# A two-layer decoder: the latent attention's context work made in the first phase and brought back from memory

## The chip, the core and the metric

The kernel runs on one core of a Trainium2 chip. The metric is the device time of one execution in microseconds (us). TensorE's granted clock has two levels, 1.2 and 2.4 GHz; the profile writes it as a share of 2.4 GHz.

## The reference, cut to what matters

Sixty-four sequences of 128 rows of 256 numbers go through two layers. What bears on the change is the attention of a second-layer sublayer, in which the running activations ask a context:

```python
x = x + mamba(layernorm(x)); x = x + cross_attention(layernorm(x), ctx)      # ctx's own keys and values
x = x + experts(layernorm(x)); x = x + causal_attention(layernorm(x))
x = x + latent_attention(ctx, layernorm(x)); x = x + ternary_layer(layernorm(x))

def latent_attention(ctx, latents):
    xn = layer_norm(ctx, ln_x_w, ln_x_b)              # depends on ctx alone
    ln = layer_norm(latents, ln_l_w, ln_l_b)
    k, v = split(concat([xn, ln]) @ Wkv)              # 8 heads of 64
    q, k = l2norm(ln @ Wq) * q_scale, l2norm(k) * k_scale
    p = softmax(where(mask, (q @ k.T) * 8, -max))
    return layer_norm((p @ v) @ Wo, ln_o_w, ln_o_b)
```

The context's half of keys and values depends on nothing that the layers compute, so it can be made at any time.

## The kernel before

The work runs in three phases. **Phase 1** loops over the 64 sequences: the state-space sublayer (chains M, V, N), the first cross attention (Y makes the context's keys and values for it, X the rest), and the router with the shared expert (F). **Phase 2** goes through 144 tiles of routed rows, expert by expert. **Phase 3** loops over the sequences again: causal attention (A), the context's norm, keys and values for the latent attention (C), the latents' norm, queries, keys and values (K), the latent attention (L), and the last part (T).

Every engine runs the same loop body over and over. A chain is a generator that stops at named steps, and a table, `ORDER`, gives for each phase and engine the order in which the steps of all chains stand in one body: "Kla0" is step la0 of chain K. Chains have depths, as `("A", A, 0), ("C", C, 1)`: in the body in which A works on sequence n, C works on sequence n-1. A body is thus one sequence's worth of each chain, 67 or so bodies make a phase, and 60 of them are the hardware loop. Engines take their steps strictly in the table's order; a step that waits holds up all that is behind it on its engine. Semaphores tie the engines together: `done(engine, name, b)` waits for a signal of sequence b, `was(...)` for the same signal of the sequence before (a buffer that has to be free).

Chain C has, in the kernel before, these steps in phase 3, all on PSUM bank Q[3]: moments of the context rows on VectorE (lnc), 1/sqrt of the variance on GpSimd, the normed rows on VectorE (lncn), two transposes on TensorE and two scaled copies on ScalarE; keys = two matmuls of 512 columns (la1, la1h), their squares on ScalarE (lq0), sums by head on VectorE, a power on GpSimd, the scaling on VectorE (lu0), four transposes (lT0) and a copy into `klT`; values = two more matmuls of 512 columns (la3, la3h) and a copy into `Vl`. Each float32 matmul of the source shows as two instructions in the trace. Chain K does the same for the latents on Q[4] and feeds the same two tiles.

Other names used below: in phase 1, "Nd0" to "Nd3" are subtractions on GpSimd over 128x1024 elements (L618), "Nm0" to "Nm2" products on VectorE of the same size (L847), "Nm3" the fourth of them on GpSimd (L622); "Vcv" to "Vcv3" are the convolution, 16 small operations on VectorE (L817, L819), "Vcth" the tanh after it on ScalarE; "Ftop" is the choice of two experts on VectorE (from L893), "Frk" the rank matmuls that wait for it, "Xs0" and "Xs2" the scores of the cross attention, "Xm0" to "Xm3" their maxima and exponentials, "Xt2" and "Xt3" the transposes of the exponentials and the copies (L1162), "Xpv" the products with the values (L1440), "Nx1" the sum that ends the state-space sublayer (L861).

## Time and profile before

| | us |
|---|---|
| median of 3 runs | 4805.45 (4796.27 to 4813.17) |
| profiled execution | 4825.85 |
| its span, first to last instruction | 4824.2 |
| mean granted TensorE clock | 0.956 |

The 40 slices of the page show phase 1 up to about 2510 us, phase 2 to about 2800 us, and phase 3 from there to the end. In phase 1 TensorE is busy for eight tenths of nearly every slice, in phase 3 for nine tenths or more. "PE" is TensorE, "PEld" its weight loads, "DVE" VectorE, "ACT" ScalarE, "POOL" GpSimd and "SP" SyncE; "PEclk" is the granted clock.

### The profile page before, as it was taken

The numbers are of one execution on the slowest core, as the hardware profiler recorded it, in microseconds if no ns is written. First come the engines' busy times: TensorE is split into PE (matmuls) and PEld (weight loads), VectorE is DVE, ScalarE is ACT, GpSimd is POOL, SyncE is SP. The second block draws the span as 40 slices with busy tenths as digits, with TensorE's granted clock in tenths as the row PEclk, the third lists the DMA queues.
The fourth block names the chain that finished last, engine by engine and source line by source line (L and its number), as shares of the span: only waits on it lengthen the run. The fifth ranks groups of instructions, "written<-read, shape, count | busy, mean of one in ns | idle before, by whom it ended". The sixth has DMA issues, their size and how long they took to land. (4 is left out here: it accounts for less than half of the span.)

```text
span 4824.2 us, 120433 instructions
## 1 busy us (share of the span) xinstructions
PE 4196.8 (87%) x34006; PEld 3000.4 (62%) x34071; DVE 3385.8 (70%) x8668; ACT 2902.8 (60%) x7030; POOL 2741.4 (57%) x4093
## 2 busy tenths in 40 slices
...
DMA packets 215885, 304.09 MB, mean 63 GB/s; under 512 B 56608, under 2 KB 167456, under 8 KB 215840
## 3 DMA queue, kind: packets, MB, share of 16 engines
...
q8 instruction: 23, 0.38, 0.0%
q14 instruction: 22, 0.18, 0.0%
...
## 5 line engine op out<-in xcount | busy, mean ns | idle before, releaser
L1402 PE MATMUL Q<-ident,arena 128*128 128x128 f32 x4768 | 824.8, 298 | 141.0 <-ACT arena L1145 48.9
L1402 PEld LDWEIGHTS Q<-ident,arena 128*128 128x128 f32 x4768 | 570.3, 149 | 385.2 <-issue 135.8
L1397 PE MATMUL Q<-Wkvl,arena 128*128 128x512 f32 x1024 | 498.7, 599 | 0.0
L618 POOL TENSOR_TENSOR arena<-arena 128x1024 f32<-128x1024 f32 x256 | 479.6, 1890 | 6.7 <-DMA arena<-cum_rows 6.7
L682 POOL TENSOR_TENSOR l<-l,half_pow 128x8 f32<-128x8 f32 x192 | 318.8, 1661 | 230.4 <-DVE l L1025 228.8
L707 POOL TENSOR_TENSOR arena<-arena,part_of 128x512 f32<-128x512 f32 x256 | 264.1, 1043 | 188.6 <-DVE part_of L1063 187.7
L769 DVE TENSOR_REDUCE mx<-Q 128x4 f32<-128x512 f32 x512 | 343.8, 681 | 9.3 <-PE Q L1425 4.7
L1440 PE MATMUL Q<-arena 128*17 128x128 f32 x4096 | 243.2, 313 | 102.3 <-ACT arena L1162 102.2
L1431 PE MATMUL Q<-ident,arena 128*128 128x128 f32 x2048 | 300.0, 280 | 23.3 <-ACT arena L1162 18.4
L1431 PEld LDWEIGHTS Q<-ident,arena 128*128 128x128 f32 x2048 | 231.9, 141 | 132.3 <-issue 93.6
L1155 ACT ACTIVATE arena<-Q,mx 128x128 f32<-128x128 f32 x1024 | 282.6, 374 | 0.5 <-DVE mx L769 0.5
L1425 PE MATMUL Q<-arena 32*128 32x128 f32 x4096 | 281.9, 276 | 0.0
L1202 ACT ACTIVATE arena<-arena 128x1024 f32<-128x1024 f32 x256 | 268.6, 1049 | 0.1
L1199 ACT ACTIVATE arena<-arena 128x1024 f32<-128x1024 f32 x256 | 268.1, 1047 | 0.0
L1425 PEld LDWEIGHTS Q<-arena 32*128 32x128 f32 x4096 | 262.8, 189 | 3.2
L1361 ACT ACTIVATE arena<-Q,mxl 128x256 f32<-128x256 f32 x512 | 235.8, 473 | 46.2 <-DVE mxl L1058 38.9
L1497 PE MATMUL Q<-arena 128*16 128x128 f32 x4096 | 164.3, 278 | 107.6 <-DVE arena L847 98.1
L1440 PEld LDWEIGHTS Q<-arena 128*17 128x17 f32 x4096 | 146.4, 106 | 178.2 <-issue 163.8
L1162 ACT ACTIVATE arena<-Q 128x512 f32<-128x512 f32 x384 | 220.0, 589 | 56.6 <-PE Q L1431 55.8
L847 DVE TENSOR_TENSOR arena<-arena 128x1024 f32<-128x1024 f32 x192 | 233.2, 1242 | 2.9 <-ACT arena L1202 2.9
L1397 PEld LDWEIGHTS Q<-Wkvl,arena 128*128 128x128 f32 x1024 | 169.6, 190 | 103.8 <-issue 103.6
L819 DVE SCALAR_TENSOR_TENSOR arena<-arena,convw 128x128 f32<-128x128 f32 x768 | 225.8, 356 | 6.8
...
## 6 DMA issues: line engine op xcount, KB each, us to landing
arena<-cum_rows SPq DMA_DIRECT2D x256, 512.0 KB, 6.3
arena<-routed_rows SPq DMA_DIRECT2D x144, 128.0 KB, 2.1
expert_rows<-arena POOLq DMA_DIRECT2D x144, 128.0 KB, 2.0
arena<-in_x_dram SPq DMA_DIRECT2D x128, 128.0 KB, 5.1
arena<-in_ctx_dram SPq DMA_DIRECT2D x128, 128.0 KB
x_rows<-arena SPq DMA_DIRECT2D x128, 128.0 KB, 1.7
arena<-x_rows SPq DMA_DIRECT2D x128, 128.0 KB, 2.4
out_dram<-arena SPq DMA_DIRECT2D x64, 128.0 KB, 1.7
```

What stands on the lines that cost most here:

```text
L618: tell(g.tensor_tensor(E8[j], E8[j], cums[:, 8 * j:8 * j + 8].unsqueeze(2).broadcast_to([P, 8, T]), ALU.subtract), "diff")
L682: link(pool, c, b, g.tensor_tensor(l2[:, k, :], l2[:, k, :], half_pow[:, :], ALU.pow), bare=True)
L707: tell(g.tensor_tensor(both, both, part_of[:, 2 * k:2 * k + 2].unsqueeze(2).broadcast_to([P, 2, 2 * T]), ALU.mult), "Pln")
L769: largest = v.tensor_reduce(mx[:, 4 * j:4 * j + 4], pj, AX.X, ALU.max, negate=True)
L1155: last = s_.activation(S[:, j, g, :], banks[j][:, g * T:(g + 1) * T], ACT.Exp, bias=mx[:, 4 * j + g:4 * j + g + 1])
L1199: tell(s_.activation(Ew[j], Ew[j], ACT.Abs), "gap")
L1202: tell(s_.activation(Ew[j], Ew[j], ACT.Exp, scale=-1.0), "E")
L1397: last = mm(out, lhs(c), rhs(c), start=c == 0, stop=c == n - 1)
L1402: last = nc.tensor.transpose(out[:, c * P:(c + 1) * P], src[:, c * P:(c + 1) * P], ident[:, :])
L1425: last = mm(banks[j][:, g * T:(g + 1) * T], QT[r, g, :], KT[r, g // 2, :], start=False, stop=g == NG - 1)
L1431: last = nc.tensor.transpose(bank[:, g * T:(g + 1) * T], S[:, j, g, :], ident[:, :])
L1440: last = mm(bank[32 * (h % 4):32 * (h % 4) + AW + 1, h // 4 * T:(h // 4 + 1) * T], V[:, h, :], PT[:, j, g, :], start=True, stop=True)
```

## The change

All of chain C moves from phase 3 to phase 1, at depth 2, and shares bank Q[2] with chain Y there. Its keys and values are stored to two new arrays in memory by a new chain S on SyncE, one body later, and loaded in phase 3 straight into `klT` and `Vl` by two new steps of L on SyncE. The host also hands over the context with its last two axes swapped, and Y loads that in place of transposing the rows: TensorE's step YcT and ScalarE's are gone. Wkvl's load moves from the later weights to the first ones. In `ORDER` C's steps are put into phase 1 and taken from phase 3, and other steps of phase 3 change places. TensorE's step "Mcum" waits for one signal in place of another before its idle matmuls.

```diff
     1: {
         "SP": """
-            Ncb0 Ncb1 Ncb2 Yc Xm Mx Ncb3 Nx Mco Fm Fo
+            Ncb0 Ncb1 Ncb2 Sk Sv Yc Cc Xm Mx Ncb3 Nx Mco Fm Fo
         "POOL": """
-            Nd0 Nd1 Nd2 Xx1r Fln3 Xln2 Mln1 Nd3 Msp Nm3 Fsc Nyg Nrms
+            Nd0 Nd1 Nd2 Xx1r Fln3 Xln2 Mln1 Clnc Nd3 Msp Nm3 Clq0 Fsc Nyg Nrms
         "DVE": """
-            Fln3 Xln2 Nm0 Mln1 Fr Yk Ftop Mdt Fslot Msp Xm0 Xm1 Fhg Nm1 Nm2 Xm2 Xm3 Fxo Vcv Vcv1 Vcv2 Vcv3 Ny0 Vxs2 Ny1 Vcb Vxdt Vgz Nx1 Xho
+            Fln3 Xln2 Clnc Nm0 Mln1 Fr Yk Clncn Ftop Mdt Fslot Msp Xm0 Xm1 Fhg Nm1 Nm2 Xm2 Xm3 Clq0 Fxo Vcv Vcv1 Vcv2 Clu0 Vcv3 Ny0 Vxs2 Ny1 Vcb Vxdt Vgz Nx1 Xho
         "ACT": """
-            Ng0 YcT Ne0 Ng1 Fln3 Xln2 Fln3n Xmr Xln2n Mln1 Frx Mln1n Xq Mab Vbc Ne1 Ng2 Yv Fth Ne2 Ng3 FhT Ne3 Xm0 Xm1 Vxp Xm2 Mcum Xm3 NYt0 Xt0 NYt1 Xt1 Vcth Xt2
-            Xt3 Nsq XOT NyT Vtz
+            Ng0 Ne0 Ng1 Fln3 Xln2 Fln3n Xmr Xln2n Mln1 Frx Mln1n Xq Yv Mab Vbc Ne1 Ng2 Clncn Fth Ne2 Ng3 FhT Ne3 Xm0 Xm1 Vxp Clq0 Xm2 Mcum Xm3 NYt0 Xt0 NYt1 Xt1
+            ClT0 Vcth Xt2 Xt3 Nsq XOT Cla3 NyT Vtz
         "PE": """
-            YcT Yk Nv0 Fln3n Yv Xln2n Fr Mln1n Xq Vbc Mdt Frk Xs0 Fgu Fguh Vip1 Vip1h FhT Xs2 Fdn Mcum Nv1 Nv2 Xt0 Nv3 Xt1 Ny0 Xt2 VCB Ny1 Xt3 Xpv Xpv0 VxsT Xpv1
-            Xpv2 NyT Xpv3 Vz Vzh Npr Nprh XOT
+            Yk Nv0 Fln3n Yv Xln2n Fr Mln1n Xq Vbc Mdt Frk Xs0 Clncn Fgu Fguh Vip1 Vip1h FhT Cla1 Xs2 Cla1h Fdn Mcum Nv1 Nv2 Xt0 Nv3 Xt1 Ny0 Xt2 VCB Ny1 ClT0 Xt3
+            Xpv Xpv0 VxsT Xpv1 Xpv2 Cla3 NyT Xpv3 Cla3h Vz Vzh Npr Nprh XOT
     3: {
         "SP": """
-            Ax Cc Kx Lm Tx To
+            Ax Lk Lv Kx Lm Tx To
         "POOL": """
-            Ag Kx4c Kln5 Aln4 Kln6 Clnc Tlno Tln7 Klq1 Lp0 Lp1 Lp2 Clq0 Lp3 Klq2
+            Ag Kx4c Kln5 Kln6 Aln4 Tlno Tln7 Klq1 Lp0 Lp1 Lp2 Lp3 Klq2
         "DVE": """
-            Kln5 Clnc Ax3 Aln4 Kln5n Kln6 Aln4n Lmr Kln6n Tlno Clncn Tx5 Tln7 Lm0 Lm1 Taq Klq1 Ak Lm2 Lm3 Lp0 Lp1 Klu1 Am0 Am1 Am2 Am3 Lp2 Tx6 Clq0 Lp3 At0 Lt0
-            At2 Klq2 Clu0 Lt2 Aho Klu2 Ax4
+            Kln5 Ax3 Kln5n Kln6 Lmr Aln4 Kln6n Tlno Lm0 Aln4n Tx5 Tln7 Lm1 Klq1 Taq Ak Lm2 Klu1 Lm3 Lp0 Am0 Lp1 Am1 Am2 Lp2 Lp3 Am3 Lt0 At0 Tx6 Klq2 At2 Lt2 Klu2
+            Aho Ax4
         "ACT": """
-            Aln4n Kln6n Clncn Lp0 Lp1 Klq1 Aq TaT Lp2 Lp3 KlT1 Am0 Clq0 Am1 Am2 Am3 At1 Klq2 At3 Lt1 AOT Lt3 AoT ClT0 KlT2 Llo Cla3 Kla4
+            Kln6n Aln4n Klq1 Lp0 Lp1 Aq Lp2 TaT KlT1 Lp3 Am0 Klq2 Am1 Am2 Am3 At1 Lt1 At3 AOT Lt3 AoT KlT2 Llo Kla4
         "PE": """
-            Two Twoh Aln4n Ls0 Kln6n Aq Clncn Kla0 Kla0h Aqv Ak Cla1 Ls2 TaT As0 Ttern KlT1 Cla1h Lt0 As3 Lt1 Kla2 At0 At1 Kla2h At2 At3 Apv Apv0 Apv1 Apv2 Apv3
-            Lt2 Lt3 AOT Lpv0 AoT ClT0 KlT2 Apr Lpv1 Cla3 Cla3h Kla4 Kla4h
+            Two Twoh Ls0 Kln6n Kla0 Aln4n Kla0h Aq Aqv Ak Ls2 TaT As0 KlT1 Ttern Kla2 Kla2h As3 Lt0 Lt1 At0 Lt2 At1 At2 At3 Apv Apv0 Apv1 Apv2 Apv3 Lt3 AOT Lpv0
+            AoT KlT2 Apr Lpv1 Kla4 Kla4h
...
+    kl_d = nc.dram_tensor("context_keys", (NB, P, KV), F32)
+    vl_d = nc.dram_tensor("context_values", (NB, P, KV), F32)
...
+        sqc, vlc = part(512), part(512)
+        xnc, cT = sqc[:, 0:D], cut(vlc[:, 0:D], DC)
...
@@ SyncE, phase 1
+            chunks(Wkvl, wkv1)
             counts["w_first"] = n_w
...
             def Y(b):
                 yield "c"
-                was(sp, "ctxTps", b)
+                was(sp, "v0", b)
+                tell(sp.dma_start(ctxT, ctxt_d[bass.ds(b, 1)].rearrange("a (c p) t -> p (a c) t", p=P)), "ctxT_in", 16)
+
+            def C(b):
+                yield "c"
+                was(sp, "lnc_xn", b)
                 tell(sp.dma_start(ctx0, rows(ctx_d, b)), "ctx0_in", 16)
+
+            def S(b):
+                yield "k"
+                done(sp, "klT0", b)
+                tell(sp.dma_start(rows(kl_d, b), sqc), "kl_out", 16)
+                yield "v"
+                done(sp, "Vl0", b)
+                tell(sp.dma_start(rows(vl_d, b), vlc), "vl_out", 16)
...
-            program(sp, "SP", 1, (("M", M, 0), ("N", N, 1), ("Y", Y, 2), ("X", X, 2), ("F", F, 3)))
+            program(sp, "SP", 1, (("M", M, 0), ("N", N, 1), ("Y", Y, 2), ("C", C, 2), ("X", X, 2), ("F", F, 3), ("S", S, 3)))
...
@@ SyncE, phase 3
             def L(b):
+                yield "k"
+                was(sp, "Sl", b, 4)
+                tell(sp.dma_start(klT[:, :, 0:T], cut(rows(kl_d, b), 4)), "kl_in", 16)
+                yield "v"
+                was(sp, "PVl", b)
+                tell(sp.dma_start(Vl[:, 0, :], rows(vl_d, b)), "vl_in", 16)
...
@@ VectorE, phase 1
+            def C(b):
+                yield "lnc"
+                done(dve, "ctx0_in", b, 16)
+                moments("lnc", ctx0, stC, mvC, "C_DVE", b)
+                yield "lncn"
+                done(dve, "lnc_rstd", b)
+                was(dve, "kl_out", b, 16)
+                tell(v.tensor_scalar(xnc, ctx0, mvC[:, 0:1], mvC[:, 3:4], ALU.subtract, ALU.mult), "lnc_xn")
+                yield from total(0, sqc, b)
+                yield from unit(0, "kn0", sqc, Q[2], b)
...
@@ ScalarE, phase 1
-                yield "cT"
-                done(act, "ctxTps", b)
-                tell(s_.activation(ctxT, cut(Q[2][:, 0:D], DC), ACT.Copy), "ctxT")
...
+            def C(b):
+                yield "lncn"
+                was(act, "vl_out", b, 16)
+                copyT("lnc", Q[2], cT, b, lnx)
+                yield "lq0"
+                done(act, "la1", b)
+                tell(s_.activation(sqc, Q[2][:, :], ACT.Square), "latsq0")
+                yield "lT0"
+                done(act, "kT0", b)
+                tell(s_.activation(sqc, Q[2][:, :], ACT.Copy), "klT0")
+                yield "la3"
+                done(act, "la3", b)
+                tell(s_.activation(vlc, Q[2][:, :], ACT.Copy), "Vl0")
...
@@ TensorE, phase 1
                 yield "cum"
-                done(pe, "ln1_T", b)
+                done(pe, "dt_pre", b)
                 awake(Q[0][:, 0:2 * T], 5)
...
-                yield "cT"
-                done(pe, "ctx0_in", b, 16)
-                was(pe, "v0c", b)
-                was(pe, "k0c", b)
-                tell(transposes(Q[2], ctx0, DC), "ctxTps")
                 yield "k"
-                done(pe, "ctxT", b)
+                done(pe, "ctxT_in", b, 16)
+                was(pe, "Vl0", b)
                 tell(across_heads(Q[2], Wk0, ctxT), "k0")
...
+            def C(b):
+                con = lambda c: cT[:, c, :]
+                yield "lncn"
+                done(pe, "v0c", b)
+                done(pe, "k0c", b)
+                lnT("lnc", xnc, Q[2], b)
+                yield "la1"
+                done(pe, "lnc_T", b)
+                last = yield from halves("la1", Q[2][:, :], con, lambda c: Wkvl[:, c, 0:KV])
+                tell(last, "la1")
+                yield "lT0"
+                done(pe, "kn0", b)
+                tell(transposes(Q[2], sqc, 4), "kT0")
+                yield "la3"
+                done(pe, "klT0", b)
+                last = yield from halves("la3", Q[2][:, :], con, lambda c: Wkvl[:, c, KV:2 * KV])
+                tell(last, "la3")
...
@@ the same functions C are taken out of phase 3 on every engine; TensorE's L waits for the loads
-                done(pe, "klT0", b)
+                done(pe, "kl_in", b, 16)
...
-                        done(pe, "Vl0", b)
+                        done(pe, "vl_in", b, 16)
```

## Rows read from the trace of the kernel before

**Rows 1.** The page, part 1: busy time, share of the span and instructions of each engine.
```profile
PE 4196.8 (87%) x34006; PEld 3000.4 (62%) x34071; DVE 3385.8 (70%) x8668; ACT 2902.8 (60%) x7030; POOL 2741.4 (57%) x4093
```

**Rows 2.** Busy time of each engine over the loop bodies of phases 1 and 3.
```profile
201.80:2416.80 2215.00, 1815.90 (x15759) 1313.82 (x15812) 1558.43 (x4131) 1441.15 (x3128) 1414.39 (x2125) 0.94 0.25 79
...
2926.90:4733.70 1806.80, 1787.00 (x14397) 1247.56 (x14396) 1427.71 (x3422) 1117.85 (x2951) 1033.59 (x1475) 1.00 0.11 31
```

**Rows 3.** SyncE, one instruction in each loop body: first and last start, in us.
```profile
L437 SPq MOVE cum_rows<-arena x60: 29/29/29, 201.8 to 2416.8; - x60
...
L525 SPq MOVE out_dram<-arena x60: 29/29/29, 2926.9 to 4733.7; - x60
```

**Rows 4.** Waits in phase 1: who for whom, total us, times, longest.
```profile
PE Q L1440 <- ACT arena L1162: 98.6, 59, 2.5
...
PE Q L1497 <- DVE arena L847: 91.6, 59, 1.6
```

**Rows 5.** TensorE in order of time in phase 3: start us, us, group, idle before.
```profile
3626.28 3.70 PE L1397 MATMUL Q<-Wkvl,arena 128*128 128x512 f32 x8
...
3629.82 1.89 PE L1397 MATMUL Q<-Wol,arena 128*128 128x256 f32 x8
...
3633.24 0.44 PE L1402 MATMUL Q<-ident,arena 128*128 128x128 f32 x2
...
3634.41 0.38 PE L1402 MATMUL Q<-ident,arena 128*128 128x128 f32 x2
...
3634.63 1.93 PE L1397 MATMUL Q<-Wql,arena 128*128 128x512 f32 x4
...
3642.66 0.66 PE L1402 MATMUL Q<-ident,arena 128*128 128x128 f32 x4 [0.28 <-DVE arena L1030]
...
3643.15 1.02 PE L1397 MATMUL Q<-Wkvl,arena 128*128 128x512 f32 x2
```

**Rows 6.** ScalarE in order of time in phase 3.
```profile
3633.72 0.81 ACT L1140 ACTIVATE arena<-Q,lnl 128x128 f32<-128x128 f32 x2 [1.37 <-PE Q L1402]
```

**Rows 7.** Groups of instructions in phase 3: busy us, mean ns of one, idle before.
```profile
L682 POOL TENSOR_TENSOR l<-l,half_pow 128x8 f32<-128x8 f32 x177 | 293.9, 1661 | 199.3 <-DVE l L1025 197.8
...
L1030 DVE TENSOR_TENSOR arena<-Q,l 128x512 f32<-128x512 f32 x177 | 120.0, 678 | 0.0
...
L1025 DVE TENSOR_REDUCE l<-arena 128x8 f32<-128x512 f32 x177 | 119.9, 677 | 1.5 <-ACT arena L1339 1.5
...
L758 DVE BATCH_NORM_STATS2 stK<-arena 128x6 f32<-128x256 f32 x118 | 50.5, 428 | 8.9
```

**Rows 8.** VectorE in order of time in phase 1.
```profile
1117.79 0.48 DVE L861 SCALAR_TENSOR_TENSOR arena<-Q,ss,arena 128x256 f32<-128x256 f32 x1 [0.70 <-PE Q L1397]
...
1121.10 1.23 DVE L847 TENSOR_TENSOR arena<-arena 128x1024 f32<-128x1024 f32 x1
...
1126.30 0.57 DVE L894 TENSOR_TENSOR rt<-rt 128x16 f32<-128x16 f32 x1
...
1138.57 3.24 DVE L817 SCALAR_TENSOR_TENSOR arena<-arena,convw,convb 128x128 f32<-128x128 f32 x4
...
1141.84 3.55 DVE L819 SCALAR_TENSOR_TENSOR arena<-arena,convw 128x128 f32<-128x128 f32 x12
```

**Rows 9.** GpSimd in order of time in phase 1, the same body.
```profile
1124.95 1.90 POOL L618 TENSOR_TENSOR arena<-arena 128x1024 f32<-128x1024 f32 x1
...
1138.98 2.42 POOL L622 TENSOR_TENSOR arena<-arena 128x1024 f32<-128x1024 f32 x1
```

**Rows 10.** TensorE in order of time in phase 1, the same body.
```profile
1146.78 0.65 PE L1440 MATMUL Q<-arena 128*17 128x128 f32 x8 [1.74 <-ACT arena L1162]
```

**Rows 11.** A stretch of phase 1: busy time, granted clock, DMA share, GB/s.
```profile
1147.40:1150.80 3.40, 3.40 (x31) 2.21 (x32) 1.29 (x2) 0.48 (x2) 3.32 (x4) 0.52 0.97 347
```

**Rows 12.** SyncE in order of time in phase 1: the context load's issue.
```profile
1107.40 0.51 SPq L454 DMA_DIRECT2D arena<-in_ctx_dram  x1
```

**Rows 13.** DMA issues in phase 1: KB each, median us to landing.
```profile
arena<-in_x_dram SPq DMA_DIRECT2D x118, 128.0 KB, 3.9
```

More of the change, by code:

```diff
@@ L225, in two_layers @@
         S1, PT1 = (part(2048).rearrange("p (j g k) -> p j g k", j=4, g=NG) for _ in range(2))
-        ctx1, xnc, l5, xn6, x4c, x4t = (part(D) for _ in range(6))
-        cT, lT = cut(part(D), DC), cut(part(D), DC)
-        sqc, sql, qn = part(512), part(512), part(512)
-        kn = part(1024).rearrange("p (c n) -> p c n", c=2)
+        l5, xn6, x4c, x4t = (part(D) for _ in range(4))
+        lT = cut(part(D), DC)
+        sql, qn, kn = part(512), part(512), part(512)
         qlT, klT, Vl = cut(part(512), 4), part(1024).rearrange("p (m t) -> p m t", m=4), part(1024).rearrange("p (c n) -> p c n", c=2)
@@ L268, in two_layers @@
         Q = [ctx.enter_context(nc.psum_tensor(f"Q{i}", [P, 512], F32)) for i in range(8)]
-        for n in ("xa_in", "xr_in", "cum_out", "wide0", "wide1", "wide2", "wide3", "ctx0_in", "mask0_in", "meta_out", "xo_out", "meta_in", "x2s_in", "ctx1_in", "mask1_in", "x4_out", "x4t_in", "out_done"):
+        for n in ("xa_in", "xr_in", "cum_out", "wide0", "wide1", "wide2", "wide3", "ctx0_in", "mask0_in", "meta_out", "xo_out", "meta_in", "x2s_in", "mask1_in", "x4_out", "x4t_in", "out_done", "ctxT_in", "kl_out", "vl_out", "kl_in", "vl_in"):
             sig(n, 16)
@@ L501, in A @@
                 tell(sp.dma_start(x2s, rows(x2_d, b)), "x2s_in", 16)
-            def C(b):
-                yield "c"
-                was(sp, "lnc_xn", b)
-                tell(sp.dma_start(ctx1, rows(ctx_d, b)), "ctx1_in", 16)
             def K(b):
```

113 lines of the change are left out of this document (41 added, 72 removed).

## The prediction

> **What bounds the kernel now.** I read the page first: TensorE is busy for 87% of the span, more than any other engine [rows 1]. An average over three phases doesn't say what a stage is worth, so next come the windows over the two loops. In phase 3 TensorE is busy for 1787 of 1807 us, at the full clock: work taken from it there shortens the body, unless something else ends later. In phase 1 it is busy for 1816 of 2215 us at a granted clock of 0.94 (part of that busy time is itself slow), and VectorE, ScalarE and GpSimd stand at 70%, 65% and 64% [rows 2]: no engine is full, so a chain that crosses the engines must be the bound. The first and last of 60 instructions that stand once in each body give the periods: (2416.8 - 201.8) / 59 = 37.54 us in phase 1, (4733.7 - 2926.9) / 59 = 30.62 us in phase 3, 30.5 in an ordinary body [rows 3]. In phase 1 TensorE waits 1.6 us in each body for VectorE's product (Nm0) and as much for ScalarE's copies (Xt3) [rows 4].
>
> The sum is thus a race: 64 passes of chain C leave a loop that TensorE fills, and enter one that is bound by waits.
>
> **Phase 3.** In the order of TensorE's starts, eight instructions of 512 columns take 3629.82 - 3626.28 = 3.54 us; half of those are Cla3, and Cla1 is as many: 3.54 us in all. The two transposes of Clncn take 0.22 us (3634.41 to 3634.63), four transposes as in KlT1 0.49, which I take for ClT0. With gaps C costs 4.3 us of TensorE in each body, and 0.28 us of waiting for VectorE stands in it too [rows 5]. What VectorE, ScalarE and GpSimd lose by it (VectorE some 2.3 us: moments, norm, sum, scaling) was beside TensorE's work. TensorE's own work then is 30.5 - 0.3 - 4.3 = 25.9 us.
>
> The cover goes as well. Now Kla0 comes 1.4 us after the start of its transposes (3633.24 to 3634.63), and Aq and Clncn fill that time [rows 5]: ScalarE's two copies begin 0.48 us after the transposes' start and take 0.81 [rows 6]. In the new order Kla0 stands right behind Kln6n, so TensorE waits there: 3633.72 + 0.81 + 0.1 - (3633.24 + 0.27) = 1.1 us. That is a new wait that nothing in the table hides. Following the other steps through the new table in the same way I find four smaller ones: As0 behind k1c (0.15), Ttern and Kla2 behind ScalarE, which must finish Lp2 first (0.6), AOT behind the copy of the heads (0.3), Apr behind the copy of o1 (0.4); 1.5 us together at worst, none at best. I take half, as the row with the only wait of today's body (0.28) lies between. New body: 25.9 + 1.1 + 0.8 = 27.8, which is 2.7 us less. Bounds: 1.8 less (all waits and some more) to 4.6 less (none). The two loads from memory and the lost context load are SyncE's: Lv waits for the body's last product (Lpv1) with Kx, Lm and Tx behind it, but Kx waited that long before, for x4. 64 x 2.7 = 173 us saved (115 to 294).
>
> **Phase 1.** I lay the body out from Nx1 at 1117.79 (time 0) [rows 8]. One path goes round: x1, the norms, router, Ftop, rank, Xs0, then VectorE without a pause from Xm0 to the end of the convolution, tanh, Xt3, Xpv, and TensorE without a pause to the next Nx1. What stands on it counts in full; what stands beside it is free.
>
> - Clnc: two operations of 0.43 and 0.18 with a gap, 0.7 us [rows 7], ahead of Nm0, for which TensorE already waits [rows 4, 8]. The later Nv0 pushes Fr by 0.6 us: **+0.6**.
> - Clncn: one operation, near 0.42 us, ahead of Ftop. Its time comes just when GpSimd makes Nd3. The row shows what that does: L894, an operation on 16 columns, began at 1126.30 and took 0.57, to the very end of Nd3 at 1124.95 + 1.90 = 1126.85 [rows 8, 9]. Nd3 stood at 7.2 on my clock and is 0.8 us later by Clnc on GpSimd (an addition and a power), so it ends at 9.9; then comes Clncn, to 10.3, and L894 ends at 10.7 in place of 9.1: with the 0.6 above 1.6 us late, so **+1.0** more (0.4 if the two don't meet).
> - Clncn's transposes and Cla1 on TensorE go ahead of Xs2, 1.2 us of which VectorE's late arrival at Xm2 covers most: **+0.4**. Cla1h is beside the path.
> - Clq0: 0.68 us [rows 7] on VectorE between Xm3 and the convolution, and 0.3 us until ScalarE's square, which stands behind Vxp, is there: **+1.0**.
> - The first four convolution operations took 3.24 us, where twelve more of their size take 3.55 together, so 2.0 of it is a stall: they met GpSimd's Nm3 (2.42 us) [rows 8, 9]. In the new order VectorE gets there later against Nm3, and half of that stall goes: **-1.0** (0 to -2.0).
> - Clu0: 0.68 us [rows 7] ahead of Vcv3: **+0.7**. GpSimd's power for it takes 1.66 us [rows 7], behind Nm3, in the shadow of Vcv1 and Vcv2; the scatter behind it has slack.
> - ClT0 on ScalarE, ahead of Vcth: it ends 0.3 us after the convolution: **+0.3**.
> - Cla3 and Cla3h: four instructions by 0.443 us, between Xpv and Npr, where TensorE is never idle: **+1.8**.
> - The lost YcT is worth nothing: TensorE waits for Nm0 right after.
>
> Sum: 4.8 us in each body, 64 x 4.8 = 307 us (bounds: 2.0 with the stall gone and the small terms hidden, 6.5 with further slow clock).
>
> A page bears on two of these terms. The Trainium skill (SBUF — State Buffer, "Who interferes with whom") says that VectorE with two inputs in SBUF, or in a fast mode on one, and GpSimd reading SBUF lock each other out for a whole instruction; L894's row agrees. By that page Clncn, a scalar operation from SBUF to SBUF, is locked out as L894 was, and the sum is the 4.8 above; were it not, the term would be 0.4 and the sum 4.2.
>
> SyncE in phase 1: Sv waits for Vl0, made by the last steps of the body before, some 3.4 us ahead of Nx1. Behind it stand Yc, Cc, Xm, Mx and Ncb3; Yc's place was at 1107.40, 10.4 us ahead [rows 12]. So these loads now start 7 us later. A load of x takes 3.9 us in the median to land [rows 13]; the context would be there 1 to 2 us after Nx1, its moments are due at 3.3, x is due at 5.2, wide3 at 8.1. All hold, by 1 to 3 us. I cost it at nothing; if that cover is gone, VectorE waits in the path, 1 to 2 us a body.
>
> Wkvl among the first weights: the same bytes through the same engines ahead of phase 1, +1 us. The store of the last keys is waited for before phase 3, long done.
>
> **Sum.** 4825.85 - 173 + 307 + 1 = 4961 us against the profiled execution, which stands 20 us above the median; 135 us more than before, so 4940 us as a median.
>
> **The rivals.**
>
> *Phase 1 absorbs it (faster).* TensorE idles for 37.5 - 30.8 = 6.8 us in a body [rows 2, 3], more than C's 4.3. If the small insertions on VectorE fall into waits, only Cla3's 1.8 us are left: 64 x 1.8 = 115, sum 4805 - 173 + 115 + 1 = 4750. It decides when phase 1's body grows by less than 2.7 us. For it: VectorE is idle for 30% of the body. Against it: those idle times are not between Xm0 and the convolution's end.
>
> *The clock.* After the wait of 1.74 us before Xpv [rows 10] TensorE ran at 0.52 in the following 3.4 us, just in the stretch without a pause [rows 11], which costs about 1.7 us. Longer waits (Nv0's, Frk's and the one ahead of ClT0 each grow by 1 us or more) may add another such stretch: +1.5 a body, 5035 us. The Trainium skill (TensorE: Matmul & The Clock Gate, "HAM oscillation — how this bites in real kernels") tells of loops that fall back to the low clock in each pass through a wait; no row here shows it for these places. The other way, Cla3 and ClT0 fill enough to keep the clock high before Npr: -1.7 a body, 4830 us.
>
> *Phase 3 takes no new wait.* TensorE stays as full as now: -294 us, sum 4819.
>
> *The held queue.* Sv's wait makes the loads late by 1.5 us: +96, 5035 us.
>
> **How the numbers follow.** The forecast (4850 to 5000) has 0.42; phase 1 absorbs it 0.23; a further slow stretch 0.12, the slow stretch lost 0.07; phase 3 clean 0.08; held queue 0.08. A measurement of this kernel tells about 0.3%, 14 us, from no change. Faster: 0.23 and some of the two near 4820 make 0.28; within 0.3%: 0.07; slower 0.65. The range takes in the absorbing case down to its 4730 and both cases at 5035: 4730 to 5060; the likeliest one's own is 4850 to 5000.
>
> **What would show it.** In the changed profile: phase 3's body near 27.8 us, with a wait of 1.1 us before Kla0 on ScalarE's scaled copies; phase 1's body near 42.3, Clncn's operation near 1 us long at GpSimd's L618, L817's four shorter than 3.24 us together, TensorE still without a pause from Xpv to Npr, and TensorE's wait for the rank (L1570) up from 1.0 to over 2 us. A phase 1 body under 40.2 us makes the prediction wrong; so would waits on DMA in phase 1.

## The result, and the profile after

The changed kernel takes 5262.45 us in the median of four runs (5256.60 to 5263.77), the kernel before 4808.87 in the same rounds: a ratio of 1.0944, 95% interval 1.0927 to 1.0960. Forecast were 4940 us and a range of 4730 to 5060. The direction was right; the size was not, and the time lies outside the range.

The page, part 1, of the changed kernel, to be set beside [rows 1]:

```profile
PE 4419.7 (84%) x33878; PEld 3103.7 (59%) x33943; DVE 3295.9 (63%) x8668; ACT 2851.9 (54%) x6966; POOL 2763.9 (53%) x4093
```

TensorE has the same work less YcT, and is busy for 223 us longer: part of its work runs slower. The windows over the loops say where (columns as in [rows 2]: window, its length, busy time of PE, PEld, DVE, ACT and POOL, granted clock, DMA share, GB/s):

```profile
217.20:2688.00 2470.80, 2053.76 (x16467) 1468.73 (x16520) 1604.19 (x4426) 1558.42 (x3364) 1571.71 (x2361) 0.92 0.28 87
3209.40:5168.00 1958.60, 1758.25 (x13572) 1190.98 (x13571) 1293.81 (x3126) 953.26 (x2656) 898.07 (x1239) 0.92 0.14 40
```

The granted clock of phase 3 was 1.00 and is 0.92. The first and last of the two instructions that stand once in each body, as in [rows 3]:

```profile
L441 SPq MOVE cum_rows<-arena x60: 29/29/29, 217.2 to 2688.0; - x60
```

```profile
L545 SPq MOVE out_dram<-arena x60: 29/29/29, 3209.4 to 5168.0; - x60
```

Phase 1's body is (2688.0 - 217.2) / 59 = 41.88 us, 4.34 more than before (forecast: 4.8 more). Phase 3's is (5168.0 - 3209.4) / 59 = 33.20 us, **2.58 more** (forecast: 2.7 less). 64 x (4.34 + 2.58) = 443 us, and the profiled spans differ by 5262.1 - 4824.2 = 438: the two bodies are the whole of it. The error sits in phase 3.

**Phase 3.** The chain of waits of TensorE in the loop of phase 3 (total us, times, longest):

```profile
PE Q L1756 <- DVE mrow L1078: 105.7, 59, 3.6
PE Q L1417 <- ACT arena L1164: 53.0, 59, 0.9
PE Q L1417 <- ACT arena L1363: 26.7, 59, 0.5
```

The second is the wait before Kla0, 53.0 / 59 = 0.9 us a body where 1.1 was forecast; the third is Kla2's, 0.45, one of the "smaller ones". The first is new: in each of 59 bodies the scores Ls0 wait for the mask's row, 105.7 / 59 = 1.8 us. Who made that row late is seen by following one body through three engines. SyncE:

```profile
4030.94 0.59 SPq L530 DMA_DIRECT2D arena<-context_keys  x1
4036.55 0.34 SPq L533 DMA_DIRECT2D arena<-context_values  x1
4037.19 0.36 SPq L525 DMA_DIRECT2D x_rows<-arena  x1
4037.81 0.34 SPq L536 DMA_DIRECT2D mask1i<-in_mask_BxS_bk_dram  x1
```

VectorE, which turns the mask into mrow (L1078):

```profile
4041.39 0.29 DVE L1078 TENSOR_SCALAR mrow<-mask1i 128x256 bf16<-128x256 uint8 x1 [2.16 <-DMA mask1i<-in_mask_BxS_bk_dram]
```

TensorE:

```profile
4036.44 1.98 PE L1417 MATMUL Q<-Wkvl,arena 128*128 128x512 f32 x4
4038.26 1.89 PE L1417 MATMUL Q<-Wol,arena 128*128 128x256 f32 x8
4041.74 0.39 PE L1756 MATMUL Q<-mrow,onesb 1*128 1x512 bf16 x2 [1.59 <-DVE mrow L1078]
4042.06 1.46 PE L1761 MATMUL Q<-arena 64*128 64x256 f32 x8
...
4045.03 2.07 PE L1417 MATMUL Q<-Wql,arena 128*128 128x512 f32 x2 [0.90 <-ACT arena L1164]
```

SyncE issues the keys' load at 4030.94 and then stands for 5.0 us, until 4036.55: the values' load (L533) waits for Lpv1, the last reader of the old values. The store of x4 and the mask's load (L536) come after it, at 4037.19 and 4037.81. The mask lands some 3.5 us later; VectorE has been idle for 2.16 us and TensorE for 1.59 us by then. There is more in these rows than the wait: two products of Wql take 2.07 us at 4045.03, which take 1.13 where the mask is in time (e1, below). The clock in that stretch, and ahead of it:

```profile
4043.00:4046.00 3.00, 2.10 (x7) 0.79 (x4) 2.64 (x8) 0.81 (x2) 1.18 (x3) 0.50 0.00 0
```

```profile
4041.00:4042.00 1.00, 0.26 (x2) 0.09 (x2) 0.61 (x2) 0.00 (x0) 0.00 (x0) 1.00 0.07 24
4043.00:4044.00 1.00, 1.00 (x6) 0.29 (x2) 0.82 (x4) 0.00 (x0) 0.85 (x3) 0.50 0.00 0
```

So the clock had already fallen when the wait of 0.90 us began, at 4044.13: it falls behind the wait for the mask.

The kernel before shows whether the mask became late or was needed sooner:

```profile
3627.53 0.33 SPq L516 DMA_DIRECT2D mask1i<-in_mask_BxS_bk_dram  x1
```

```profile
3631.86 0.39 PE L1739 MATMUL Q<-mrow,onesb 1*128 1x512 bf16 x2
```

Counted from the products with Wkvl (3626.28 before [rows 5], 4036.44 after), the mask's load was issued at 1.25 and is issued at 1.37 us, nearly the same. Ls0 began at 5.6 us; without the wait it would now begin at 3.7 (4041.74 - 1.59 = 4040.15).

**Phase 1.** One body from L881 (the old L861, time 0, at 1027.58) to the next at 1068.90; 41.32 us, where the body of [rows 8] takes 37.33 (the next L861 starts at 1155.12). VectorE:

```profile
1031.46 1.23 DVE L867 TENSOR_TENSOR arena<-arena 128x1024 f32<-128x1024 f32 x1
...
1036.53 0.17 DVE L909 TENSOR_REDUCE rt<-Q 128x1 f32<-128x16 f32 x1 [3.18 <-PE Q L1410]
1037.08 0.93 DVE L961 TENSOR_SCALAR arena<-arena,mvC 128x256 f32<-128x256 f32 x1
...
1038.11 0.17 DVE L914 TENSOR_TENSOR rt<-rt 128x16 f32<-128x16 f32 x1
...
1046.58 0.42 DVE L935 SCALAR_TENSOR_TENSOR arena<-arena,Q 128x256 f32<-128x256 f32 x1 [1.15 <-ACT arena L1281]
...
1050.23 1.29 DVE L789 TENSOR_REDUCE mx<-Q 128x4 f32<-128x512 f32 x2 [0.50 <-PE Q L1445]
1051.92 0.69 DVE L947 TENSOR_REDUCE l<-arena 128x8 f32<-128x512 f32 x1 [0.40 <-ACT arena L1292]
...
1052.86 1.13 DVE L837 SCALAR_TENSOR_TENSOR arena<-arena,convw,convb 128x128 f32<-128x128 f32 x4
...
1056.37 0.69 DVE L952 TENSOR_TENSOR arena<-Q,l 128x512 f32<-128x512 f32 x1
```

L909 is the router's first operation. In the body before it stands as:

```profile
1125.30 0.17 DVE L889 TENSOR_REDUCE rt<-Q 128x1 f32<-128x16 f32 x1 [2.30 <-PE Q L1390]
```

GpSimd and TensorE in the same body of the changed kernel:

```profile
1031.52 1.22 POOL L602 TENSOR_TENSOR mvX<-mvX,eps 128x1 f32<-128x1 f32 x1
...
1035.96 1.90 POOL L638 TENSOR_TENSOR arena<-arena 128x1024 f32<-128x1024 f32 x1
```

```profile
1032.74 1.06 PE L1517 MATMUL Q<-arena 128*16 128x128 f32 x16 [2.88 <-DVE arena L867]
...
1034.21 1.71 PE L1410 MATMUL Q<-Wv,arena 128*128 128x256 f32 x4
...
1042.66 3.46 PE L1417 MATMUL Q<-Wsgu,arena 128*128 128x512 f32 x4
1045.96 1.95 PE L1410 MATMUL Q<-arena,Win 128*128 128x128 f32 x16
...
1060.03 0.62 PE L1460 MATMUL Q<-arena 128*17 128x128 f32 x8 [1.81 <-ACT arena L1186]
...
1061.96 1.12 PE L1417 MATMUL Q<-Wkvl,arena 128*128 128x512 f32 x2
```

### The profile page after: what moved, and what is told of

It reads as the page before. It is cut to its first block, busy times and chain, and to the rows that moved or that the text cites. A ratio compares the mean times of both kernels' runs of the same rounds, so it can differ in the third digit from the quotient of the medians.

```text
span 5262.1 us, 120973 instructions
## 1 busy us (share of the span) xinstructions
PE 4419.7 (84%) x33878; PEld 3103.7 (59%) x33943; DVE 3295.9 (63%) x8668; ACT 2851.9 (54%) x6966; POOL 2763.9 (53%) x4093
## 4 chain that ended last, share of the span: by engine, by line
PE 67%; DVE 11%; issue 8%; DMA 5%; ACT 4%; POOL 2%; SPq 1%; DVEq 1%; POOLq 0%; ACTq 0%
PE Q L1417 19%; PE Q L1422 12%; PE Q L1410 11%; PE Q L1445 4%; DMA mask1i<-in_mask_BxS_bk_dram 4%; PE Q L1451 4%; PE Q L1460 3%; PE Q L1761 3%; PE Q L1517 2%; PE Q L1632 2%; DVE arena L867 1%; PE Q L1644 1%; PE Q L1794 1%; PE Q L1756 1%; POOL arena L714 1%
## 5 line engine op out<-in xcount | busy, mean ns | idle before, releaser
L1422 PE MATMUL Q<-ident,arena 128*128 128x128 f32 x4640 | 817.2, 295 | 128.8 <-ACT arena L1169 49.0
L1422 PEld LDWEIGHTS Q<-ident,arena 128*128 128x128 f32 x4640 | 549.5, 148 | 442.2 <-issue 185.4
L1417 PE MATMUL Q<-Wkvl,arena 128*128 128x512 f32 x1024 | 537.8, 627 | 29.5 <-ACT arena L1363 29.4
L672 POOL TENSOR_TENSOR l<-l,half_pow 128x8 f32<-128x8 f32 x192 | 332.4, 1731 | 367.0 <-DVE l L947 364.9
L638 POOL TENSOR_TENSOR arena<-arena 128x1024 f32<-128x1024 f32 x256 | 479.8, 1891 | 7.4 <-DMA arena<-cum_rows 7.3
L789 DVE TENSOR_REDUCE mx<-Q 128x4 f32<-128x512 f32 x512 | 343.6, 682 | 103.9 <-PE Q L1445 103.9
L1517 PE MATMUL Q<-arena 128*16 128x128 f32 x4096 | 178.0, 296 | 188.6 <-DVE arena L867 188.5
L1460 PE MATMUL Q<-arena 128*17 128x128 f32 x4096 | 215.2, 276 | 106.9 <-ACT arena L1186 106.9
L1451 PE MATMUL Q<-ident,arena 128*128 128x128 f32 x2048 | 295.3, 277 | 3.1 <-ACT arena L1179 2.4
L1417 PE MATMUL Q<-Wql,arena 128*128 128x512 f32 x256 | 234.6, 1017 | 57.5 <-ACT arena L1164 57.5
L947 DVE TENSOR_REDUCE l<-arena 128x8 f32<-128x512 f32 x192 | 131.1, 683 | 194.8 <-ACT arena L1359 168.8
L1410 PEld LDWEIGHTS Q<-arena,Win 128*128 128x128 f32 x1536 | 217.6, 217 | 56.4 <-issue 52.2
L1517 PEld LDWEIGHTS Q<-arena 128*16 128x16 f32 x4096 | 110.2, 100 | 237.8 <-DVE arena L867 220.0
L1451 PEld LDWEIGHTS Q<-ident,arena 128*128 128x128 f32 x2048 | 230.0, 141 | 31.8 <-issue 26.2
```

The lines of the kernel that those rows point to most:

```text
L638: tell(g.tensor_tensor(E8[j], E8[j], cums[:, 8 * j:8 * j + 8].unsqueeze(2).broadcast_to([P, 8, T]), ALU.subtract), "diff")
L672: link(pool, c, b, g.tensor_tensor(l2[:, k, :], l2[:, k, :], half_pow[:, :], ALU.pow), bare=True)
L789: largest = v.tensor_reduce(mx[:, 4 * j:4 * j + 4], pj, AX.X, ALU.max, negate=True)
L1410: last = mm(out, lhs(c), rhs(c), start=c == 0, stop=c == n - 1)
L1417: last = mm(out, lhs(c), rhs(c), start=c == 0, stop=c == n - 1)
L1422: last = nc.tensor.transpose(out[:, c * P:(c + 1) * P], src[:, c * P:(c + 1) * P], ident[:, :])
```

## The experiments

They ran on three chips (e1 to e4, e5 to e8, e9 to e12), on each of which the kernel before took 4827 to 4830 us; each ratio is to the kernel before on the same chip. "P1" and "P3" are the periods of the two bodies, worked out as above; "clock" is the granted clock over the loop of phase 3 (for e6 to e8: of phase 1).

| kernel | us | ratio to before, 95% | P1 | P3 | clock |
|---|---|---|---|---|---|
| e5, the changed kernel again | 5242.1 | 1.0853 (1.0835 to 1.0871) | 41.87 | 32.96 | 0.92 |
| e1, mask's load early | 4954.6 | 1.0263 (1.0246 to 1.0280) | 41.04 | 29.06 | 1.00 |
| e2, values' load late | 5144.2 | 1.0652 (1.0634 to 1.0669) | 41.08 | 32.00 | 0.94 |
| e3, old order of phase 3 | 5063.4 | 1.0487 (1.0469 to 1.0504) | 41.08 | 30.70 | 0.96 |
| e4, e3 and mask early | 5052.3 | 1.0470 (1.0448 to 1.0492) | 41.04 | 30.52 | 0.97 |
| e10, TensorE kept busy | 5074.0 | 1.0505 (1.0487 to 1.0522) | 41.07 | 30.94 | 0.99 |
| e9, e1 and Ls0 between | 4962.2 | 1.0272 (1.0255 to 1.0290) | 41.04 | 29.24 | 1.00 |
| e6, e1 and values' products last | 4879.7 | 1.0111 (1.0094 to 1.0128) | 39.75 | 29.10 | 0.97 |
| e7, e1 and moments later | 4941.5 | 1.0233 (1.0216 to 1.0250) | 40.78 | 29.08 | 0.94 |
| e8, e1 and norm later | 5070.7 | 1.0505 (1.0487 to 1.0522) | 42.86 | 29.10 | 0.90 |
| e11, e6, e7 and e9 together | 4887.1 | 1.0121 (1.0104 to 1.0138) | 39.94 | 29.18 | 1.00 |
| e12, before with turned context | 4827.0 | 0.9995 (0.9986 to 1.0005) | 37.55 | 30.62 | 1.00 |

**The theory** after the result: in phase 3 the mask's load is too late for Ls0, which the new order puts ahead of Aln4n and with C's products no longer in front; the idle time then brings the clock down. **Rivals**: the hand-made order of steps is bad by itself; or the loads of keys and values are late.

**e1_mask_early.** The mask's load goes ahead of the values' load and of x4's store.

```diff
-            Ax Lk Lv Kx Lm Tx To
+            Ax Lk Lm Lv Kx Tx To
```

> The changed kernel with one move on SyncE in phase 3: the mask's load (Lm) goes ahead of the load of the values (Lv) and the store of x4 (Kx). Theory 'late mask': VectorE's 2.2 us wait for the mask, TensorE's 1.6 us wait behind it and the slow clock after it go; phase 3's body falls from 33.2 to 29 to 30 us, the time to 5000 to 5080 us. Rival 'the new order of steps': the body is bound by the steps' order, the mask's wait turns into another, and the time stays within 40 us of 5262.

SyncE in phase 3 of e1:

```profile
4016.79 0.39 SPq L533 DMA_DIRECT2D mask1i<-in_mask_BxS_bk_dram  x1
4021.54 0.33 SPq L536 DMA_DIRECT2D arena<-context_values  x1
4022.18 0.36 SPq L525 DMA_DIRECT2D x_rows<-arena  x1
```

The waits of TensorE over its loop of phase 3:

```profile
PE Q L1417 <- ACT arena L1164: 52.9, 59, 0.9
PE Q L1417 <- ACT arena L1363: 26.6, 59, 0.5
PE Q L1756 <- DVE mrow L1078: 3.0, 2, 2.7
```

and TensorE in time, around Kla0:

```profile
4025.39 1.14 PE L1761 MATMUL Q<-arena 64*128 64x256 f32 x8
...
4027.79 1.13 PE L1417 MATMUL Q<-Wql,arena 128*128 128x512 f32 x2 [0.90 <-ACT arena L1164]
...
4036.98 1.98 PE L1417 MATMUL Q<-Wkvl,arena 128*128 128x512 f32 x4 [0.45 <-ACT arena L1363]
```

The mask is issued 5.4 us ahead of x4's store, mrow is waited for twice in 59 bodies, the clock is back at 1.00, and the same two products of Wql take 1.13. The body goes from 32.96 (e5) to 29.06. The time was forecast at 5000 to 5080 us and comes out lower, since phase 1, whose code is the same, has 0.8 us less a body as well; that part is looked at under e6. In phase 3 that one row of the table of steps is worth 3.9 us a body, some 240 us of the 415 that the change costs (e5); the two profiles differ by 242 us behind the end of phase 1's loop and by 49 ahead of it. Forecast for phase 3's body had been 27.8; more on the other 1.26 below.

With the mask in time the change costs 127 us, where the prediction had 135. That this is so close is luck: 29.06 + 41.04 and the forecast 27.8 + 42.3 are both 70.1, with phase 3 1.3 us above its forecast and phase 1 as much below.

**e2_values_late.** Values' load behind the store and the mask (`Ax Lk Kx Lm Lv Tx To`).

> The changed kernel with the load of the values (Lv) moved on SyncE behind the mask's (Lm), which stays behind the store of x4 (Kx). If Lv's wait for the body's last product holds the mask back, the time falls as in the run with the mask ahead of both (about 5040 us). If the store Kx holds it, which waits for x4 anyway and was issued 0.6 us after Lv's in the trace, nothing changes: 5230 to 5265 us, some us less for the load that no longer travels ahead of the mask.

It asks which of the two stands in the mask's way. The time lies between the two that were forecast. The body falls by only 1.0, to 32.00, and TensorE still waits for mrow in 59 bodies, 82.8 us. The wait for Lpv1 is the smaller part; x4's store, which waits for x4 itself, is nearly as late. Before the change the mask stood behind the same store, and TensorE waited for it once in 59 bodies, since Ls0 came later.

**e3_old_order, e4_old_order_mask_early.** Phase 3's steps in the order of before, less those of C, on VectorE, GpSimd, ScalarE and TensorE; SyncE as in the change (e3) and as in e1 (e4).

```diff
-            Two Twoh Ls0 Kln6n Kla0 Aln4n Kla0h Aq Aqv Ak Ls2 TaT As0 KlT1 Ttern Kla2 ...
+            Two Twoh Aln4n Ls0 Kln6n Aq Kla0 Kla0h Aqv Ak Ls2 TaT As0 Ttern KlT1 Lt0 ...
```

> The changed kernel with phase 3's steps on TensorE, VectorE, ScalarE and GpSimd in the order of the kernel before, context steps left out; SyncE as in the change. Theory 'late mask': the old order takes the mask later (Lmr behind the norm of the causal attention) but without the context's work it is still early: a part of the wait stays, body 29 to 32 us, time 4990 to 5180. Rival 'the new order of steps' is the cause of the lost gain: body 27 to 28, time 4860 to 4920 us.

> Both: the old order of steps without the context's, and the mask's load ahead of Lv and Kx. If the order costs nothing, this equals the run with the mask ahead alone (about 5040 us). If the steps put by hand cost the wait before Kla0 that the prediction found (1.1 us a body), this one is 50 to 90 us faster than it: 4950 to 4990 us. TensorE alone needs 25.9 us a body, which would be 4800 us.

TensorE's waits in phase 3 of e3:

```profile
PE Q L1422 <- DVE arena L782: 82.5, 59, 4.7
PE Q L1422 <- DVE arena L952: 44.5, 59, 0.9
...
PE Q L1756 <- DVE mrow L1078: 5.3, 13, 0.7
```

e3 falls in the range of the late mask; e4 was forecast to equal e1 or to be the faster of the two, and is 98 us slower. With the old order the late mask costs nearly nothing (30.70 against 30.52): it is waited for in 13 bodies. So the mask's place costs 3.9 us a body in the new order and 0.2 in the old one. The old order has waits of its own, 1.4 us a body before Aln4n's transposes and 0.75 before KlT1's. With the mask in time the new order is the better one, by 30.52 - 29.06 = 1.46 us a body; with the mask as late as in the change it is the worse one, by 32.96 - 30.70 = 2.26. The rival "the order is bad by itself" is out, and so are late keys or values, for which TensorE waits in none of these traces.

**e5_same.** The changed kernel again, on the second chip.

> The changed kernel once more, unaltered, on the chip of the runs below. Phase 1's body was 41.9 us in its first profile and 41.0 us in the profiles of the four runs before this one, which have the same phase 1. If that is the chip's or the run's doing, this one may show 41.0 too and 5215 us; if it came from the code, 41.9 and 5262 us.

The time is 0.4% below its first measurement, most of it in phase 3; phase 1's period is the same to 0.01 us, so 41.9 was no accident of one run.

**e10_kept_busy.** The mask as late as in the change; TensorE makes six products into an unused bank ahead of the waits of Ls0.

```diff
                 yield "s0"
+                awake(Q[3][:, :], 6)
                 done(pe, "kl_in", b, 16)
```

> The changed kernel, mask's load as late as it was, with six idle products of TensorE (results unused) at the head of Ls0, ahead of its waits. It separates the wait for the mask from the slow clock behind it. The changed kernel takes 33.2 (33.0 in its second run) in a body of phase 3 and e1 29.06: 4.0 us, of which the trace shows 1.8 as idle time of TensorE before Ls0. If the rest is the lower clock that follows the idle time, the granted clock of phase 3 goes from 0.91 to 0.93 back to near 1.00 and the body to 30 to 31, the kernel to 5070 to 5130. If the rest comes from the order of loads itself (values and keys late, their buffers), the clock may rise but the body stays at 32.5 to 33.5 and the kernel at 5230 to 5280.

The window over its loop of phase 3:

```profile
3157.90:4983.40 1825.50, 1703.50 (x13864) 1162.08 (x13922) 1292.19 (x3126) 952.33 (x2655) 891.56 (x1238) 0.99 0.15 43
```

and TensorE's wait for mrow there, behind the six products:

```profile
PE Q L1756 <- DVE mrow L1078: 29.1, 55, 2.2
```

The six products end before the mask is there in 55 of 59 bodies, so they don't hold up Ls0. The clock is back at 0.99 and the body at 30.94, both as forecast for the slow clock. The cost of the late mask, 32.96 - 29.06 = 3.9 us a body, thus falls in two: 1.9 of waiting (30.94 - 29.06), which fillers can't take away, and 2.0 of slow clock behind it, which they can. 0.8 in phase 1 comes on top, as in e1 to e4 (see e6).

**e6_values_at_end.** On e1; in phase 1 the products of the context's values (Cla3, Cla3h) go behind the last step of the body, their copy to the end of ScalarE's (whose XOT also goes behind NyT and Vtz), and both stores behind Nx.

```diff
 SP
-            Ncb0 Ncb1 Ncb2 Sk Sv Yc Cc Xm Mx Ncb3 Nx Mco Fm Fo
+            Ncb0 Ncb1 Ncb2 Yc Cc Xm Mx Ncb3 Nx Sk Sv Mco Fm Fo
 PE
-            Xpv Xpv0 VxsT Xpv1 Xpv2 Cla3 NyT Xpv3 Cla3h Vz Vzh Npr Nprh XOT
+            Xpv Xpv0 VxsT Xpv1 Xpv2 NyT Xpv3 Vz Vzh Npr Nprh XOT Cla3 Cla3h
```

> The run with the mask ahead (4955 us), and in phase 1 the context's values (Cla3, Cla3h) at the end of TensorE's body, behind Npr and XOT, their copy at the end of ScalarE's, and the stores Sk and Sv behind Nx on SyncE. Theory of the path: they leave the stretch without a pause from Xpv to Npr (1.8 us) for the wait before Nv0 (2.9 us): 1.5 to 2.5 us less in each body, 4800 to 4860 us. Rival 'TensorE's share': phase 1 is bound by its total work and the time stays within 25 us of 4955. Rival 'queue': the loads that stood behind Sv come earlier and give a gain of their own; then no wait on DMA goes, since none is there.

The best version: 1.29 us off phase 1's body, where 1.5 to 2.5 had been forecast; the time, 4879.7 us, lies above the forecast too. The products now stand where TensorE waits for Nm0. Its waits in phase 1 of e6:

```profile
PE Q L1586 <- DVE selb L922: 114.1, 59, 1.9
...
PE Q L1517 <- DVE arena L867: 62.2, 59, 1.1
```

Nm0 (L867) is waited for 62.2 us in place of 175.6 in e1, and the clock over the loop is 0.97 in place of 0.92 to 0.93. From Xpv to Nx1 the mean body has 7.2 us in place of 9.0, just the 1.8 of the four instructions. Ahead of Xpv 0.4 us is lost: the router's first operation comes 0.4 earlier, but Clncn (L961) then stands in the lock with Nd3 for longer, 1.81 us on average in place of 1.13, and ends no earlier; the wait for the rank (L1586) is 114.1 us in place of 38.1. Where the slow clock sat is read from three groups of products, mean ns of one over the loop of phase 1:

| products | before | after | e1 | e6 | e12 |
|---|---|---|---|---|---|
| Wv, behind Nv0 | 380 | 516 | 537 | 380 | 406 |
| Wsgu (Fgu) | 744 | 932 | 678 | 833 | 934 |
| heads by values, behind Xpv (L1440, now L1460) | 357 | 276 | 276 | 276 | 349 |

The slow stretch behind Xpv is gone in every version that makes Cla3, and one behind Nv0 has come. The table also tells apart the two values of P1 in code that is the same, 41.87 (after, e5) and 41.04 to 41.08 (e1 to e4, e9, e10): Wsgu's busy time is 185.2 us in after and 129.7 in e1, 0.94 us a body. Why Fgu falls into the slow stretch in one and not in the other isn't settled. The chip isn't ruled out: e5 ran on another one than e1 to e4, e9 and e10. But it can't be all, for e11, on the chip of e9 and e10, has 920 ns.

**e7_moments_later, e8_rows_later.** On e1, VectorE's steps of the context's norm in phase 1 put elsewhere: the moments behind Nm0 and Mln1 (e7); the norm itself (Clncn) behind Ftop, Mdt, Fslot and Msp (e8), out of reach of GpSimd's Nd3.

```diff
-            Fln3 Xln2 Clnc Nm0 Mln1 Fr Yk Clncn Ftop Mdt Fslot Msp Xm0
+            Fln3 Xln2 Nm0 Mln1 Clnc Fr Yk Clncn Ftop Mdt Fslot Msp Xm0      (e7)
+            Fln3 Xln2 Clnc Nm0 Mln1 Fr Yk Ftop Mdt Fslot Msp Clncn Xm0      (e8)
```

> The run with the mask ahead (4955 us), and in phase 1 the context's moments (Clnc) on VectorE behind Nm0 and Mln1 in place of ahead of them. Theory of the path: Nm0 is 0.7 us earlier and no longer meets GpSimd's first operation of the second norm (1.22 us in place of 0.19): 0.6 to 1.6 us less in each body, 4850 to 4915 us. Rival: Clnc was in VectorE's idle time anyway; within 20 us of 4955.

> The run with the mask ahead (4955 us), and in phase 1 the context's normed rows (Clncn) on VectorE behind Msp, ahead of Xm0, in place of ahead of Ftop. There GpSimd has no 1.9 us operation: the 0.9 to 1.1 us that it takes become 0.4, still on the path: 0.5 us less in each body, 4915 to 4935 us. Rival 'no lock': it costs the same in both places, within 15 us of 4955.

e7 takes 0.26 us off the body, and its 4941.5 us lie within the 20 us of the rival. But the moments weren't in idle time: Nm0 comes 0.67 us earlier on average, L602 takes 0.19 us as the theory had it, and the routing's L914 ends 0.53 earlier. Behind it 0.33 of that is lost at Fgu, whose Wsgu products take 835 ns in place of 678 in e1. So the 0.6 put down for the moments nearly holds, and the slow clock took back more than half of it. e8 makes the body 1.82 worse, outside both of its forecasts. TensorE's waits in phase 1 of e8:

```profile
PE Q L1517 <- DVE arena L867: 175.3, 59, 3.1
...
PE Q L1422 <- DVE arena L961: 58.8, 59, 1.2
```

The second is new: Clncn's transposes stand ahead of Fgu on TensorE, so they wait 1.0 us a body for L961, with Fgu and what needs it behind them; and Fgu's products then take 1007 ns in place of 678, 1.2 us a body. The two overlap, and no run parts them. L961 takes 0.48 us there and 1.13 in e1: the lock with GpSimd, 0.65 us, is the cheaper of the two places.

**e9_scores_between.** On e1, Ls0 between Kln6n and Kla0 (`Two Twoh Kln6n Ls0 Kla0 Aln4n ...`).

> The kernel of e1 with one more move: in phase 3 TensorE makes the transposes Kln6n before the scores Ls0, so that the products Kla0, which wait for ScalarE's copy of Kln6n's transposes, no longer stand right behind them with nothing between. In e1 TensorE waits for that copy in 55 of 59 bodies, 49.3 us, 0.9 a body. If that wait is idle time on the path, Ls0 covers it: 29.06 goes to some 28.4 to 28.7 a body and the kernel from 4954.6 to 4915 to 4935 us. If another engine sets the body by now (the rival), the wait turns up elsewhere: 28.9 to 29.2, 4945 to 4965.

Its waits in phase 3:

```profile
PE Q L1422 <- DVE arena L782: 45.2, 59, 3.8
```

The wait before Kla0 is gone, and 45.2 / 59 = 0.77 us before the transposes of a norm (L782) has come in its place: nothing is won. That was the rival, with 29.24 us near its 28.9 to 29.2 and a time inside its range.

**e11_all_three.** e6 with the steps of e7 and e9.

> e6 (values of the context last in phase 1, mask early in phase 3), with the moments of the context's norm put behind Nm0 and Mln1 (e7, which took 0.26 off a body of phase 1) and Ls0 between Kln6n and Kla0 (e9). If the three gains add, 4879.7 goes down by 0.2 to 0.3 times 64 and 0.3 to 0.6 times 64: 4825 to 4850 us, level with the kernel before (4827 to 4828). If they stand for one and the same wait, it stays at 4870 to 4885.

It is no better than e6: the three gains don't add. Nm0 comes no earlier than in e6 (4.53 us behind Nx1 in both, on average), and its 4887 us are 2 above the range that was forecast for gains that don't add; Wsgu's products take 920 ns in place of 833. No version measured here beats the kernel before.

**e12_turned_alone.** The kernel before with the turned context loaded in place of YcT's transposes and copy, and nothing else.

> The kernel before with one part of the change alone: the turned context loaded in place of the context in phase 1, and TensorE's four transposes and ScalarE's copy of them (YcT) gone. The prediction put this at nothing, since ScalarE and TensorE have slack where YcT stands: 4815 to 4840 us and a body of 37.4 to 37.7 then. If TensorE's 0.3 us and the wait that goes with it lie on the path: 37.0 to 37.2 and 4795 to 4810. If the wait for the load or a lower clock makes it worse: 38 and more, 4855 and more.

4827.0 against 4829.5 us, the interval on both sides of 1, both periods as before. The part costs nothing and brings nothing, as forecast. (TensorE has two matmul instructions less for each sequence, not four: 33878 in place of 34006 in the whole change.) Wsgu's 934 ns a product (744 before) don't reach the period here. They needn't come from the edit: on this chip 12 of 13 runs of the kernel before have a mean clock of 0.940 to 0.943, as e12 has, and about the time of the run at 0.952.

## Why the prediction was wrong, step by step

**The step that failed** is the sentence on SyncE in phase 3: "Lv waits for the body's last product (Lpv1) with Kx, Lm and Tx behind it, but Kx waited that long before, for x4." It asks whether the loads come later than before, and finds: hardly. It doesn't ask whether the work that needs them comes earlier. It does: C's products and Aln4n no longer stand ahead of Ls0, nor Aln4 and others ahead of Lmr. The rows above show it: the mask's load 0.1 us later, Ls0 1.9 us sooner. The forecast followed each step of TensorE's new table to the engine that feeds it, and Ls0 not on to VectorE's mrow and the mask's landing. Cost: 3.9 us a body where nothing was put down (e5 against e1), 1.9 waiting and 2.0 slow clock (e10).

**The clock in phase 3** stood nowhere in the prediction; it was weighed for phase 1 alone, since phase 3 ran at 1.00 throughout [rows 2]. Behind the idle 1.59 us the clock fell to 0.50 within 1.3 us, ahead of the 0.90 us wait, and in the trace it falls within 3 us of the end of the mask's wait in 53 of the 59 bodies; with e1's waits of 0.90 and 0.45 alone it stays at 1.00. The Trainium skill (TensorE: Matmul & The Clock Gate, "HAM oscillation — how this bites in real kernels") describes a loop that falls back to the low clock in each pass behind a wait for a DMA. The trace agrees as to the pattern, in those 53 bodies: waiting for the mask's DMA, by way of VectorE, 0.92 over the loop, and 1.00 with the wait gone.

**Phase 3's other terms**, read from e1: the wait before Kla0 0.90 us (forecast 1.1); C's TensorE work gone as counted. The term "half of 1.5 us of small waits" was mis-sized. The body of e1 at 4025.39 takes 4054.32 - 4025.39 = 28.93 us. Taking starts to starts, without C and the wait of 0.28 the body before has 30.51 - 4.25 - 0.28 = 25.98 us; e1 adds 1.06 before Kla0, 0.46 before Kla2, 0.74 in three groups of transposes that wait for their inputs a little each, and 0.7 in products that run longer right behind such gaps. Without the first that is 1.9 us, where 0.8 was taken and 1.5 given as the worst of them.

**Phase 1** came out at +4.34 against +4.8, in the two runs of the changed kernel, and the body read above goes term by term:

| term | forecast | read in that body |
|---|---|---|
| Clnc ahead of Nm0 | +0.6 | Nm0 at 3.88 in place of 3.31: +0.57 |
| Clncn locked out by Nd3 | +1.0 | L914 (old L894) ends at 10.70 in place of 9.08: +1.62 with the line above |
| Fgu in a slow stretch | a rival, +1.5 | wait of 1.15 before L935 for ScalarE's L1281, none before: +1.24 |
| Clncn's transposes and Cla1 ahead of Xs2 | +0.4 | wait of 0.50 before L789 at 1050.23: +0.6 |
| Clq0 | +1.0 | wait 0.40 and 0.60: +1.0 |
| stall of the convolution | -1.0 | four operations 1.16 start to start, 3.27 before: -2.1 |
| Clu0 | +0.7 | +0.61 |
| ClT0 | +0.3 | to Xpv +0.53 |
| Cla3, Cla3h | +1.8 | 2 x 0.96, less 1.29 of slow clock lost: +0.6 |

The column read adds up to 4.1 us, and 41.32 - 37.33 is 4.0. L961 took 0.93 us, till just behind the end of Nd3 (1035.96 + 1.90 = 1037.86), near the 1 us named beforehand; over the loop it takes 1.22 on average. The router's L909 was 1.44 us late already (8.95 on the body's clock, 7.51 before): 0.57 from Nm0, and 0.87 from TensorE's slow clock behind Nv0's wait. In this body the second part costs nothing, since Clncn ends with Nd3 in any case. Fgu took 3.30 us start to start (1042.66 to 1045.96) where it had taken 1.82 and began 0.39 later behind Clncn's transposes; 1.24 of these 1.87 us reached VectorE. So six of the terms held within 0.25 us. Three were out by 1.1 to 1.2: the stall of the convolution, Cla3, and the slow stretch at Fgu, which the sum didn't have. That they cancel is luck. The last two are the rivals for the clock, one slow stretch more and one lost. One of the signs failed: the wait for the rank went to 76.5 / 59 = 1.3 us, not over 2. e6 shows that Cla3's cost isn't the 1.8 us of its instructions but their place: at the end of the body they fill a wait. The held queue (Sv 6.6 us behind Sk) cost nothing: no engine waits for a DMA in phase 1's new loads, as forecast.

**Sum.** The forecast had 64 x (33.20 - 27.8) = 346 us too little in phase 3 and 64 x (4.8 - 4.34) = 29 too much in phase 1. That is 317, against 5262 - 4940 = 322. (Wkvl among the first weights was forecast at +1; the first store L441 came 3.1 us later.)
